# Two bias additions in a macaron layer pair: from GpSimd tensor operations to accumulating transfers

## What is computed

```python
x = x + 0.5 * _L0_ffn_ref(_layernorm(x), ...)     # int8-quantized 128x128 product, plus a bias row
x = x + _L0_attn_ref(_layernorm(x), ...)          # conv, gated linear recurrence, gated FFN
x = x + 0.5 * _L0_ffn_ref(_layernorm(x), ...)     # the quantized product again
x = x + 0.5 * _L1_ffn_ref(_layernorm(x), ...)     # shared expert, and top 2 of 8 routed experts
x = x + _L1_attn_ref(_layernorm(x), ...)          # gated linear attention; ends with "@ Wo + bo"
x = x + 0.5 * _L1_ffn_ref(_layernorm(x), ...)     # the experts again
```

## Time and profile before

| | |
|---|---|
| median of 3 runs | 807.21 us |
| profiled execution | 805.45 us, of which the span is 802.4 us |
| mean granted TensorE clock | 0.953 of full speed |
| busy: PE, DVE, ACT, POOL | 647.6, 512.9, 396.1, 385.1 us |
| PE busy in 60 to 172, 172 to 262 us | 103.85 of 112, 74.69 of 90 us |
| PE busy in 262 to 430, 430 to 560 us | 147.18 of 168, 103.71 of 130 us |
| DMA busy share in 0 to 60, 262 to 430 us | 0.98, 0.57 |

### The profile page before, as it was taken

The page is one execution under the profiler, slowest core; times in us unless marked ns, Lnnn a source line. Parts: engine busy times, 40 slices in busy tenths (PEclk is TensorE's granted clock), DMA queues, the critical chain, the costliest instruction groups (busy, mean ns, idle before and its releaser), DMA issues.

```text
span 802.4 us, 14619 instructions
## 1 busy us (share of the span) xinstructions
PE 647.6 (81%) x4312; PEld 508.4 (63%) x4312; DVE 512.9 (64%) x1704; ACT 396.1 (49%) x975; POOL 385.1 (48%) x401
## 2 busy tenths in 40 slices
PE   1377999996789888897896679899899998877850
PEld 0234556455457677796884467768777997766840
DVE  5879868667788466364233897977854874742315
ACT  1267687984964634543452606255247324434430
POOL 3327345246655167677562412174634733574540
PEclk9997999998999999999999699999999999999985
DMA  9992000000313246566775300013343343446839
GB/s 333 411 411 94 1 1 1 1 14 21 103 30 91 62 110 180 159 188 199 215 230 143 90 1 1 2 55 107 111 135 104 117 121 103 119 133 181 236 127 290
DMA packets 73566, 100.98 MB, mean 126 GB/s; under 512 B 10417, under 2 KB 45105, under 8 KB 73233
## 3 DMA queue, kind: packets, MB, share of 16 engines
q1 hardware_dynamic: 64848, 82.21, 34.3%
q0 software_dynamic: 8640, 17.84, 6.1%
HBM read 61.79 MB, written 38.23 MB: 125 GB/s over the span
## 4 chain that ended last, share of the span: by engine, by line
PE 51%; DVE 12%; POOL 10%; issue 10%; DMA 7%; ACT 6%; SPq 3%; POOLq 0%; DVEq 0%; ACTq 0%
PE bank L971 10%; POOL rows_by_expert L769 6%; PE bank L952 5%; PE bank L1171 4%; PE bank L290 4%; PE bank L629 3%; PE bank L464 3%; PE bank L615 3%; PE bank L866 2%; PE bank L852 2%; DMA tin<-rows_by_expert 2%; PE bank L644 2%; PE bank L841 2%; PE bank L295 2%; DMA rows_done<-tout,tin 2%
## 5 line engine op out<-in xcount | busy, mean ns | idle before, releaser
L971 PE MATMUL bank<-tint,twt 128*128 128x128 f32 x1136 | 153.6, 279 | 8.1 <-DVE thidt L1010 7.9
L769 POOL DMA_INDIRECT rows_by_expert<-xx,sidx x128 | 125.7, 982 | 71.3 <-DVE xx L752 35.5
L971 PEld LDWEIGHTS bank<-tint,twt 128*128 128x128 f32 x1136 | 140.3, 194 | 10.4 <-DVE thidt L1010 9.7
L1021 POOL DMA_INDIRECT rows_done<-tout,tin x98 | 95.1, 970 | 100.7 <-ACT tout L994 79.0
L1010 DVE TENSOR_TENSOR thidt<-tsil,bank 128x256 f32<-128x256 f32 x142 | 58.9, 419 | 106.5 <-ACT tsil L989 75.6
L952 PE MATMUL bank<-e_dn,thidt 128*128 x568 | 90.8, 283 | 18.8 <-issue 14.2
L952 PEld LDWEIGHTS bank<-e_dn,thidt 128*128 128x128 f32 x568 | 77.3, 193 | 40.1 <-issue 39.9
L989 ACT ACTIVATE tsil<-bank 128x256 f32<-128x256 f32 x142 | 54.5, 384 | 89.7 <-PE bank L971 89.4
L982 ACT ACTIVATE tint<-bank 128x128 f32<-128x128 f32 x142 | 39.3, 277 | 88.7 <-PE bank L958 88.3
L1171 PE MATMUL bank<-bufA,bufB 128*128 128x128 f32 x448 | 62.2, 288 | 8.0 <-DVE at L1196 3.8
L1171 PEld LDWEIGHTS bank<-bufA,bufB 128*128 128x128 f32 x448 | 56.5, 200 | 12.6 <-DVE tseg L1193 6.4
(11 more groups left out here) (253 smaller groups left out, 1387.7 us busy)
## 6 DMA issues: line engine op xcount, KB each, us to landing
twt<-moe_gu SPq DMA_DIRECT2D x142, 256.0 KB
rows_by_expert<-tout SPq DMA_DIRECT2D x25, 715.0 KB, 20.1
tin<-rows_by_expert SPq DMA_DIRECT2D x142, 65.0 KB, 2.5
hid<-rows_done SPq DMA_DIRECT2D x24, 256.0 KB, 4.8
x<-x_in SPq DMA_DIRECT2D x4, 512.0 KB, 6.8
rows_by_expert<-xx,sidx POOLq DMA_INDIRECT x128
out<-x SPq DMA_DIRECT2D x8, 256.0 KB, 4.8
rows_done<-tout,tin POOLq DMA_INDIRECT x98, 2.4
```

The costliest lines, as they stand in the source:

```text
L769: pool.indirect_dma_start(out=rows_by_expert, out_offset=bass.IndirectOffsetOnAxis(ap=sidx[h][:, k:k + 1], axis=0), in_=xx[h][:, r, t, :], ...
L971: m = pe.matmul(bank[UP_BANKS[p][j]][:, c * P:(c + 1) * P], weights[:, c * P:(c + 1) * P], tint[g % TURNS][:, :], start=True, stop=True)
L1021: pool.indirect_dma_start(out=rows_done, out_offset=bass.IndirectOffsetOnAxis(ap=dst, axis=0), in_=tout[:, g % RING, :], in_offset=None).t ...
```

## The change

Both additions become transfers from GpSimd's queue that accumulate into x: the source is the bias row of the partition, repeated four times by a step of 0, the destination the unit's 256 KB. Such a transfer counts 16 on its semaphore when it has landed. There are two semaphores, one for even and one for odd units, shared by the 16 transfers of the one kind and the 8 of the other. So that no two transfers on one semaphore are under way, unit u waits until the reader of unit u - 2 is through (`s_xq` or `s_x`). A count on `s_carry`, for which nobody waits, goes before each transfer, as before the indirect ones.

```diff
         def q_bias_gpsimd(pool, u, p):
             pool.wait_ge(s_qmul, n(u, p))
-            pool.tensor_tensor(xg(u), xg(u), half_qb[:, None, :].to_broadcast([P, TILES, P]), ALU.add).then_inc(s_qxb, 1)
+            if n(u, p) > 2:
+                pool.wait_ge(s_xq, n(u, p) - 2)
+            pool.sem_inc(s_carry, 1)
+            pool.dma_start(xg(u), half_qb[:, None, :].to_broadcast([P, TILES, P]), accum_op=ALU.add).then_inc(s_biased[u % 2], 16)
...
         def q_out_vector(dve, u, p):
             dve.wait_ge(s_qy, n(u, p))
-            dve.wait_ge(s_qxb, n(u, p))
+            dve.wait_ge(s_biased[u % 2], 16 * ((n(u, p) + 1) // 2))
...
         def g_bias_gpsimd(pool, u):
             pool.wait_ge(s_gxn, n(u))
-            pool.tensor_tensor(xg(u), xg(u), rows[:, None, R_BO:R_BO + P].to_broadcast([P, TILES, P]), ALU.add).then_inc(s_xbo, 1)
+            if u >= 2:
+                pool.wait_ge(s_x, n(u) - 2)
+            pool.sem_inc(s_carry, 1)
+            pool.dma_start(xg(u), rows[:, None, R_BO:R_BO + P].to_broadcast([P, TILES, P]), accum_op=ALU.add).then_inc(s_biased[u % 2], 16)
...
         def g_add_vector(dve, u):
             dve.wait_ge(s_op, n(u))
-            dve.wait_ge(s_xbo, n(u))
+            dve.wait_ge(s_biased[u % 2], 16 * (UNITS + u // 2 + 1))
...
             q_bias_gpsimd(pool, 6, 0)
+            f_b_gpsimd(pool, 2)
             q_bias_gpsimd(pool, 7, 0)
-            f_b_gpsimd(pool, 2)
...
             r_scatter_gpsimd(pool, 0, 1, 1)
+            g_bias_gpsimd(pool, 4)
             r_scatter_gpsimd(pool, 1, 1, 0)
```

More of the change, by code:

```diff
@@ L209, in macaron_kernel @@
         s_qve = sem("s_qve"); s_qroot = sem("s_qroot"); s_qmul = sem("s_qmul"); s_qi = sem("s_qi"); s_qtr = sem("s_qtr")
-        s_qit = sem("s_qit"); s_qy = sem("s_qy"); s_qxb = sem("s_qxb"); s_xq = sem("s_xq")
+        s_qit = sem("s_qit"); s_qy = sem("s_qy"); s_xq = sem("s_xq")
         s_fve = sem("s_fve"); s_fr1 = sem("s_fr1"); s_frstd = sem("s_frstd"); s_t = sem("s_t"); s_ttr = sem("s_ttr")
@@ L241, in macaron_kernel @@
         s_cross = sem("s_cross"); s_cc = sem("s_cc"); s_o = sem("s_o"); s_oc = sem("s_oc"); s_op = sem("s_op")
-        s_xbo = sem("s_xbo"); s_x = sem("s_x"); s_out = sem("s_out")
+        s_biased = [sem(f"s_biased{h}") for h in range(2)]; s_x = sem("s_x"); s_out = sem("s_out")
         FIRST, LOADS = 5, 6
@@ L2274, in _ @@
             r_root_gpsimd(pool, 0, 1)
-            g_bias_gpsimd(pool, 4)
             g_root_gpsimd(pool, 3)
-            g_bias_gpsimd(pool, 5)
             r_scatter_gpsimd(pool, 0, 1, 0)
             r_scatter_gpsimd(pool, 0, 1, 1)
+            g_bias_gpsimd(pool, 4)
             r_scatter_gpsimd(pool, 1, 1, 0)
@@ L2282, in _ @@
             r_root_gpsimd(pool, 1, 1)
-            g_bias_gpsimd(pool, 6)
-            g_bias_gpsimd(pool, 7)
+            g_bias_gpsimd(pool, 5)
             r_scatter_gpsimd(pool, 2, 1, 0)
@@ L2288, in _ @@
             r_scatter_gpsimd(pool, 3, 1, 1)
-            for j in range(0, 8):
+            for j in range(0, 7):
                 t_store_gpsimd(pool, 1, j)
+            g_bias_gpsimd(pool, 6)
+            t_store_gpsimd(pool, 1, 7)
+            g_bias_gpsimd(pool, 7)
             r_root_gpsimd(pool, 2, 1)
```

## The result

The changed kernel takes 829.13 us (median of 4 runs, 825.14 to 832.42) against 806.37 for the kernel before (4 runs): a ratio of 1.029, 95% interval 1.025 to 1.033. The direction was forecast, the size was not: 829 lies above the range, and the likeliest case had +6.6 us where +22.8 came. The profiled execution took 830.06 us (span 827.8, granted clock 0.935 where it was 0.953).

A forecast was written before the change was run, and what follows sets the result against it. No engine was taken to bound the whole; the chain was half TensorE. The late pair's 5.3 us plus 1.3, half of the smaller terms, gave +6.6 on 805.45, plus 1.76 to the median: about 814 us, range 804 to 825.

The forecast's parts named there:

- g, the start: Units 0 to 2, first pass: landings hidden or about 0.1 us late beside the zero fills; counted as nothing.
- Rival 3: Zero fills hold up the transfers of units 0 to 2: landing 11 us, +7 beside the 6.6, 821 us; chance 0.10.
- Landing elsewhere: Time from issue of a new transfer until its semaphore stands: taken as 4.8 us, ends 2.6 and 8.
- Issue: GpSimd's time to issue one new transfer: taken as 1.3 us, near the indirect transfers.
- a and b, the late pair: Units 6 and 7, second pass: VectorE's readers wait and the stores at 309.15 and 319.20 come late; +5.3 us together.
- Rival 4: Waits hidden: the 5.3 us are absorbed at the next wave's gate, +1 to +2, 809 us; chance 0.16.
- c: Unit 4 of line 1076, issued between two runs of scatters: the scatter behind it +0.7 us.
- d: Unit 7, first pass: issue waits for unit 5's reader, so f_xh behind it starts 0.7 us later.
- e: Units 4 and 5, second pass: the first's reader 1.1 us late, say +0.6 for TensorE's transposes.
- f: GpSimd's bias additions at 67.96 and 179.51 in the chain of waits: 0.25 and 0.4 us for the issue, +0.65.
- Relief of VectorE: VectorE no longer held up by GpSimd additions, at the start and at 236 us: counted as 0.
- rival 1: Landing 2.6 us, issue 0.96, with VectorE gaining 1.9 us at the start: 805.7 us, not slower; chance 0.14.

The follow-up runs named there:

- experiments with rows and fills: Changed kernel with the quantized product's bias rows of 2 KB (806.37 us) or 1 KB (816.29 us), or with zero fills cut smaller (813.34 us) or held back (808.31 us).
- the plain transfer: Changed kernel, but transfers of units 0 to 3 of the first pass write the bias row over x instead of adding it: 807.63 us, one run.
- without the start: Changed kernel with units 0 to 3 of the first pass back as GpSimd tensor additions, the other 20 staying transfers: 803.74 us, ratio 0.999.
- the start alone: Kernel before with only units 0 to 3 of the first pass as transfers, the other 20 staying GpSimd additions: 824.07 us, ratio 1.020.
- late fills: Changed kernel with the 25 zero fills held back until unit 5's reader of the first pass: 808.31 us, ratio 1.005.
- rows of 1 KB: Changed kernel with two bias rows side by side as the quantized product's source, 256 pieces of 1 KB per transfer: 816.29 us, ratio 1.014.

## Why the prediction was wrong

The failed step is **g, the start**, which I counted as nothing. It read "transfer issued at 17.95, lands at 22.8: hidden by VectorE's own work", with a landing of 4.8 us from a row without the fills beside it, and noted the full engines only in its last sentence. The landings there were 14.5 us for unit 0, 21.1 for unit 1 and 14.05 for unit 2. The chain shows how they add up: unit 1's reader comes at 40.61 instead of 28.47 (+12.1), and unit 2's, which waits again, at 67.18 instead of 45.88 (+21.3).

**Rival 3** had the mechanism, down to the 32 pieces per engine, at a chance of 0.10. It was mis-sized in two terms; what follows is worked out after the result. It took 0.19 us of waiting for each piece; from the 4.1 us of an unloaded landing to 14.05 are 9.9 us over 33 packets, 0.30 each. And it priced unit 0 alone, as if each transfer had the engines to itself: units 0 and 1 are issued 1.65 us apart, and their 66 packets per engine drain from 17.79 to 40.5, 0.34 us each, the fixed part of a landing included. With both, unit 1 lands at 17.8 + 66 x 0.34 = 40.2, 11.7 us after the 28.47 of its reader. Unit 2, issued at 40.34 before, would land at 54.4, 8.5 us after its reader's 45.88, and all of this comes 11.7 later: +20, which is 827.

The Trainium skill (DMA: Bandwidth & Descriptors, Queues, rings and completion order) says that each DMA engine takes turns between its queues packet by packet, and puts typical packets at 9 to 17 descriptors. The experiments with rows and fills agree with the first half (14.05 us at 33 packets, 8.79 at 9, 9.41 at 33 beside smaller ones). The second does not hold for accumulating transfers here: 528 packets for 512 pieces are one piece to a packet, and the plain transfer, with 80, has about eight.

**Landing elsewhere** (L): taken 4.8, measured 3.9 to 5.7 away from the fills, in the middle 4.1. Nearly right. **Issue** (g): taken 1.3, measured 1.40. Right.

**a and b, the late pair, +5.3**: wrong by the step "all 3.8 us go through". The reader was 3.74 us late, and the stores 0.2 and 0.6 us. I took the store at 309.15 for one that waits for ScalarE, because the chain has a tout just before it. By the count of tiles that tout (308.50) is tile 13's and the store is tile 9's, which had been ready for 10 us; what came last before it was no condition of it. In b I did the same: the tout at 316.55 is that of tile 16 and not of tile 12, stored at 319.20. Rival 4 (hidden after all) was right in what came of this pair, but not in the place: the wait ends in GpSimd's late queue, not at a gate for loads.

**c**: the scatter behind unit 4's transfer was to come 0.7 us later after the output addition of unit 2. In the changed kernel it is 548.27 to 550.55, 2.28 us, against 1.72: +0.56. Right in size, and lost in the gain of that stretch. **d**: +0.7 forecast, none found at its place. `f_xh` starts 0.83 us after the start of the issue, not after its end, 1.41 us behind unit 5's reader, where it was 1.39. **e**: the reader of unit 4 of the second pass waits for TensorE in the changed kernel; where the start is not late (without the start) it does wait 1.15 us for its transfer, the 1.1 of the forecast. **f** came in part: the offset of `f_b` goes from 20.1 at unit 3 to 20.7 at unit 4 and from 20.7 at unit 5 to 21.2 at unit 6, the 0.4 that stood there. Without the start it makes the same two steps, and with the start alone it stays at 21.3 to 21.4, so the 20 other transfers cost about 1 us there. It is not seen in the whole.

**Relief of VectorE**, counted 0: it is 1.6 us at the start where the transfers land early (late fills), near the 1.9 of rival 1, and about 3 us in the attention of layer 1, which no part of the prediction had. In the changed kernel the first is lost under the waits. The second shows as the fall from +22.2 to +18.3, but the last store is at +25.9. Of these 7.6 us 4.5 arise between two stores, at 718.73 and 732.30 before and at 740.76 and 758.76 here. TensorE in that stretch:

| | stretch | TensorE busy | granted clock |
|---|---|---|---|
| before | 718.7 to 732.3, 13.6 us | 9.51 us | 1.00 |
| changed | 740.7 to 758.8, 18.1 us | 14.36 us | 0.72 |

From 748 to 758 us the granted clock was 0.50, that is 1.2 GHz, after TensorE had stood idle for 1.98 us before 747.01, and eight products of L974 took up to 1.92 us instead of some 1.1. TensorE was busy for 8.24 of these 10 us; at the full clock half of that would be saved, 4.1 us by this estimate. So nearly all of the 4.5 us is TensorE's clock in the profiled execution. The kernel with rows of 1 KB has the same step (its offset goes from 7.4 to 11.9 us, with a granted clock of 0.65 from 730 to 740 us), the one with the four transfers alone has none. Why the clock fell there, and the other 3 us, stay open.

## What to carry to other kernels

Price a transfer by the packets per engine and by who else is on the engines while it is under way, not by its bytes and a landing from a quiet stretch; two in line pay for each other. An accumulating transfer from GpSimd with a source row repeated by a step of 0 should be given the longest contiguous row that the buffers allow. And before a delay is carried through a store, look how old its input is when the store is issued.

## What the runs showed of the hardware

The landing of a 256 KB transfer of GpSimd beside the fills grew with its packets per engine: 7.3 us at 5 (plain), 8.8 to 8.9 at 9, 11.2 to 11.3 at 17 and 14.1 to 14.5 at 33 (changed kernel) for the first of two; 7.3, 10.4 to 10.6, 14.4 to 14.6 and 17.7 to 21.1 for one issued some 1.5 us behind another. With the four transfers alone 33 packets took up to 15.2 and 22.2. Away from the fills the one with 33 took 3.9 to 5.7 and the one with 9 mostly 3.2 to 3.5. The growth is less than in proportion: for the first of two 0.4 us a packet from 5 to 9, 0.3 to 17 and 0.2 to 33; why is open.

An accumulating direct transfer puts each contiguous piece into a packet of its own (528, 272 and 144 packets for 512, 256 and 128 pieces), a plain one about eight (80 for 512).

The issue on GpSimd goes by pieces, but weakly: 1.40 us for 512, 1.31 for 256, 0.94 for 128, and 0.78 for the plain one. A tensor operation behind it starts 0.83 us after its start.
